# Three feed-forward products of a transformer kernel, taken as sums of products of rounded parts

## The reference

```
x = x + attn(layernorm(x))          # block A: 16 heads, relative bias, causal
x = x + xattn(layernorm(x), ctx)    # block B and D: 8 heads, attends to ctx
x = x + ffn(layernorm(x))           # block C and the last part: 8 experts, one per row
...
y = y @ Wo + x                      # in attn
z = _rms_norm(y, ln2_w)
z = jax.nn.relu(z @ W1) @ W2        # W1 256x1024, W2 1024x256
return z + y
...
ffn = jax.nn.relu(q_enh @ ffn_w1 + ffn_b1) @ ffn_w2 + ffn_b2   # in xattn
```

## Time and profile before

| | us |
|---|---|
| median of 3 runs | 1431.43 (1429.8 to 1434.38) |
| the profiled execution, own time | 1430.63 |
| its span, first to last instruction | 1428.8 |
| PE busy | 1275.9 (89%) |
| DVE busy | 766.8 (54%) |
| ACT busy | 583.0 (41%) |
| POOL busy | 390.7 (27%) |

### The profile page before, as it was taken

How to read it: one execution, slowest core, us unless ns; L and a number is a source line. 1 busy time by engine, 2 the same in 40 slices (tenths; PEclk the granted TensorE clock), 3 DMA queues, 4 the chain that set the end, 5 groups by cost and what they waited for, 6 DMA issues and landing times.

```text
span 1428.8 us, 27261 instructions
## 1 busy us (share of the span) xinstructions
PE 1275.9 (89%) x8838; PEld 929.8 (65%) x8839; DVE 766.8 (54%) x2053; ACT 583.0 (41%) x1253; POOL 390.7 (27%) x680
## 2 busy tenths in 40 slices
PE   6588999999999999999999999999987449999997
PEld 4365776767777776767777777767765325555554
DVE  5645566676766666676666666676643241121111
ACT  3424436363545536363544536363522212222221
POOL 2311121212141221213141221213122124444443
PEclk9598999999999999999999999999999669999999
DMA  8300000000000000000000000000054002112111
GB/s 273 97 8 9 16 1 31 1 29 0 29 29 0 29 0 29 0 29 0 29 29 0 29 0 29 0 29 22 2 192 177 30 22 62 53 56 60 59 55 38
DMA packets 44135, 56.69 MB, mean 40 GB/s; under 512 B 6486, under 2 KB 38016, under 8 KB 44097
## 3 DMA queue, kind: packets, MB, share of 16 engines
q1 hardware_dynamic: 37824, 41.23, 8.8%
q0 software_dynamic: 5616, 14.43, 3.5%
q10 hardware_dynamic: 656, 0.52, 0.1%
HBM read 40.44 MB, written 16.65 MB: 40 GB/s over the span
## 4 chain that ended last, share of the span: by engine, by line
PE 75%; DVE 10%; ACT 8%; issue 5%; POOL 1%; DMA 0%; ACTq 0%; DVEq 0%; SPq 0%; POOLq 0%
PE bank L1337 69%; PE bank L1372 2%; ACT a_p L725 2%; ACT shared L730 2%; PE bank L1519 2%; DVE a_p L1140 2%; DVE shared L1114 1%; PE bank L1664 1%; DVE a_sq L1108 1%; ACT shared L759 1%; ACT b_qh L659 1%; DVE a_split L1084 0%; DVE a_split L1083 0%; DVE shared L1291 0%; DVE a_split L1082 0%
## 5 line engine op out<-in xcount | busy, mean ns | idle before, releaser
L1337 PE MATMUL bank<-shared 128*128 128x256 f32 (+4 forms) x2242 | 447.8, 380 | 44.9 <-ACT shared L670 13.8
L1337 PEld LDWEIGHTS bank<-shared 128*128 128x128 f32 (+2 forms) x2242 | 318.1, 173 | 125.5 <-issue 31.5
L1140 DVE TENSOR_TENSOR a_p<-a_p,eb 128x385 f32<-128x385 f32 x256 | 126.2, 556 | 89.5 <-ACT a_p L725 89.5
L1337 PE MATMUL bank<-up,shared 128*128 x312 | 144.5, 606 | 11.0 <-issue 11.0
L725 ACT ACTIVATE a_p<-bank 128x385 f32<-128x385 f32 x256 | 105.1, 503 | 42.0 <-PE bank L1337 41.9
L869 POOL TENSOR_SCALAR a_rz<-a_ms 128x2 f32<-128x2 f32 x16 | 3.1, 191 | 431.7 <-ACT a_sq L736 431.7
L1337 PE MATMUL bank<-a_xnT,w 128*128 128x256 f32 x512 | 114.7, 382 | 1.4 <-ACT a_xnT L622 1.4
L1337 PE MATMUL bank<-w,a_hT 128*128 128x256 f32 x512 | 113.1, 379 | 0.0
L1314 DVE TENSOR_TENSOR shared<-bank,shared 128x512 f32<-128x512 f32 x39 | 27.0, 692 | 154.4 <-ACT shared L757 84.7
L622 ACT COPY a_xnT<-bank 128x512 f32<-128x512 f32 x32 | 18.8, 587 | 220.2 <-PE bank L1372 220.2
L1337 PEld LDWEIGHTS bank<-a_xnT,w 128*128 128x128 f32 x512 | 96.0, 190 | 18.1 <-issue 3.4
(11 more groups left out here) (206 smaller groups left out, 2037.9 us busy)
## 6 DMA issues: line engine op xcount, KB each, us to landing
up<-in_L_ffn_up_w SPq DMA_DIRECT2D x8, 1024.0 KB, 14.4
x_in<-in_x SPq DMA_DIRECT2D x16, 256.0 KB, 2.7
shared<-in_ctx SPq DMA_DIRECT2D x16, 256.0 KB, 3.0
rows_x<-shared SPq DMA_DIRECT2D x16, 256.0 KB, 2.9
rows_skip<-shared SPq DMA_DIRECT2D x16, 256.0 KB, 3.1
down<-in_L_ffn_down_w SPq DMA_DIRECT2D x8, 512.0 KB, 12.5
toep<-a_hT SPq DMA_DIRECT2D x1, 3072.0 KB, 10.2
eb<-toep SPq DMA_DIRECT2D x4, 512.0 KB, 6.2
```

Source lines behind the costliest of these rows:

```text
L1140: tt(a_p[:, n_ % NPA], a_p[:, n_ % NPA], eb[:, n_], ALU.mult).then_inc(sig["a_p"], 1)
L1337: return mm(out, lhsT=lhsT, rhs=rhs, start=first, stop=last, **kw)
```

## The change

W1 and W2 of block A (w01, w02) and the first feed-forward weight of the cross block (w11) are split into a float32r part (`w_hi`) and a rest (`w_low`), likewise their inputs (`a_zT`, `a_hT`, `d_qT`), and each float32 product becomes three float32r products, from turn 3 on (SPLIT_FROM = 3). `w12` stays as it is.

- The weights' high parts are written over the weights themselves. There is no room to keep the rests: they are computed once in turn 2 in scratch room (`made0`, `a_hT_low`), stored to DRAM, and loaded again in every turn, 1024 KB each, into room that is free at that time: w01's rest over the queries and keys, w02's over `a_p`, w11's over `b_p`.
- Setup: ACT rounds two weights aside in turn 2 ahead of its scores (2048 columns each), the third at the end of turn 2, then writes w11's high part (two halves); at the head of turn 3 it waits until all three rests are stored; ahead of the scores of turn 3 it writes the high parts of w01 and w02 (four halves). DVE computes the rests after ACT has rounded.
- In each turn DVE gets six more operations, 128x512 each: the rest of `d_qT`, of `a_zT` and of the four pieces of `a_hT` (the last with the ReLU in the same instruction). ACT's operations on these jobs now write the high parts. The bank is freed by DVE.
- A.h0 to A.h3 get four banks (1, 2, 3, 0) in place of two.

```diff
-    add((2, 3), [f"A.h{n}" for n in range(4)])
+    add((1, 2, 3, 0), [f"A.h{n}" for n in range(4)])
+SPLIT = ("w11", "w01", "w02",)
+SPLIT_FROM = 3
...
# SP, in turn
+            if it.first == SPLIT_FROM - 1:
+                for n, name in enumerate(SPLIT):
+                    sp.wait_ge(s_low, n + 1)
+                    sp.dma_start(low_of[name].ap(), made_low[n % 2].bitcast(F32)).then_inc(s_low_out[name], 16)
+                for name in SPLIT:
+                    sp.wait_ge(s_low_out[name], 16)
...
+            if "A" in it.stages and it.first >= SPLIT_FROM:
+                full(sp, it, f"A.s{H0 - 1}")
+                sp.dma_start(flat(w01_low[:]).bitcast(F32), low_of["w01"].ap()).then_inc(s_low_in["w01"], 16)
+                after(sp, "a_p_used", it.batch("A"))
+                sp.dma_start(flat(w02_low[:]).bitcast(F32), low_of["w02"].ap()).then_inc(s_low_in["w02"], 16)
+            if "B" in it.stages:
+                after(sp, "b_p_used", it.batch("B"))
+                sp.dma_start(flat(w11_low[:]).bitcast(F32), low_of["w11"].ap()).then_inc(s_low_in["w11"], 16)
...
# ACT
+        def round_aside(which):
+            for n in which:
+                if n == 0:
+                    act.wait_ge(s_w, 4 * C + 3)
+                if n == 2:
+                    act.wait_ge(s_low_out[SPLIT[0]], 16)
+                copy(made_low[n % 2], flat(weight[SPLIT[n]][:])).then_inc(s_hi, 1)
+        def round_in_place(names):
+            act.wait_ge(s_low, len(SPLIT))
+            for name in names:
+                for half in range(2):
+                    part = slice(half * HID, (half + 1) * HID)
+                    copy(flat(weight_hi[name][:])[:, part], flat(weight[name][:])[:, part]).then_inc(s_round, 1)
...
+            if it.first == SPLIT_FROM:
+                for name in SPLIT:
+                    act.wait_ge(s_low_out[name], 16)
             if A:
                 evacuate(it, "A.xn", a_xnT[:].rearrange("p c s -> p (c s)"))
...
+            if it.first == SPLIT_FROM - 1:
+                round_aside((0, 1))
+            if it.first == SPLIT_FROM:
+                round_in_place(SPLIT[1:])
             for what, st, n in PLAN:
...
# DVE
+        def low_parts(which):
+            for n in which:
+                dve.wait_ge(s_hi, n + 1)
+                tt(made_low[n % 2], flat(weight[SPLIT[n]][:]), made_low[n % 2].bitcast(F32), ALU.subtract).then_inc(s_low, 1)
+        def rest(it, job, dst, hi, name, n=None):
+            ps = full(dve, it, job)
+            first = SPLIT_FROM - 1 if name[0] == "a" else 0
+            wait(dve, sig[name], (it.batch("D" if name == "d_qhi" else "A") - first) * PER_BATCH[name] + (n or 1))
+            if n:
+                ins = dve.scalar_tensor_tensor(flat(dst), ps[:], 0.0, flat(hi).bitcast(F32), ALU.max, ALU.subtract)
+            else:
+                ins = tt(flat(dst), ps[:], flat(hi).bitcast(F32), ALU.subtract)
+            ins.then_inc(e_sem(job), 1)
...
# PE
+        def split_cols_out(it, job, xT, xT_low, w, w_low, first_chunk, hi_ready=None):
+            ps = claim(pe, it, job)
+            for m in range(2):
+                at = slice((first_chunk + m) * P, (first_chunk + m + 1) * P)
+                for c in range(C):
+                    product(ps[:, m * S:(m + 1) * S], w[:, c, at], xT[:, c, :], c == 0, False)
+                for c in range(C):
+                    product(ps[:, m * S:(m + 1) * S], w_low[:, c, at], xT[:, c, :], False, False)
+                if m == 0 and hi_ready:
+                    taken(pe, it, hi_ready)
+                for c in range(C):
+                    ins = product(ps[:, m * S:(m + 1) * S], w[:, c, at], xT_low[:, c, :], False,
+                                  c == C - 1)
+            ins.then_inc(f_sem(job), 1)
...
+                        if it.first >= SPLIT_FROM:
+                            product(out, a_hT_hi[:, j, tok(t)], w02_hi[:, j, :], j == 0, False)
+                            product(out, a_hT_hi[:, j, tok(t)], w02_low[:, j, :], False, False)
+                            ins = product(out, a_hT_low[:, j, tok(t)], w02_hi[:, j, :], False, j == J - 1)
```

More of the change, by code:

```diff
@@ L45 @@
 TILES_MAX = NT + E - 1
-SHARED = 22980
+SHARED = 23040
 QUARTERS = 4
@@ L238, in _build @@
     s_fold = sem("bias_through_hidden_weights")
-    shared = sbuf(ctx, "shared", [P, SHARED])
+    b_kh, b_kl, b_qh, b_ql = (sbuf(ctx, name, [P, C, S], F32R) for name in ("b_kh", "b_kl", "b_qh", "b_ql"))
+    b_nmT = sbuf(ctx, "b_nmT", [P, C, S], F32R)
+    whole_shared = ExitStack()
+    shared = sbuf(whole_shared, "shared", [P, SHARED])
+    place = {}
     def carver():
@@ L351, in _build, with doubles @@
[L351 to L354, removed]
+    def doubles(stack, sizes, wanted):
+        made, at = {}, 0
+        for name, words in sizes:
+            if name not in wanted:
+                sbuf(stack, f"under_{name}", [P, words])
+                continue
+            alias, shape = wanted[name]
+            made[alias] = sbuf(stack, alias, shape, F32R)
+            if words > C * HID and name != "made0":
+                sbuf(stack, f"above_{name}", [P, words - int(np.prod(shape[1:]))])
+        return made
@@ new lines, in _build @@
+    starts = sorted((place[name], name) for name in place)
+    sizes = [(name, nxt - at) for (at, name), (nxt, _) in zip(starts, starts[1:] + [(SHARED, None)])]
+    at_f = [name for name, _ in sizes].index("b_f")
+    sizes[at_f:at_f + 3] = [("made0", C * HID)]
+    whole_shared.close()
+    r1 = doubles(ctx, sizes, {
+        "w11": ("w11_hi", [P, C, HID]), "b_zT": ("d_qT_hi", [P, C, S]), "b_yT": ("d_qT_low", [P, C, S]),
+        "b_p": ("w11_low", [P, C, HID]), "b_hT": ("a_hT_low", [P, J, S]), "made0": ("made0", [P, C, HID])})
@@ L466, in _build @@
     pa.close()
+    pr = ExitStack()
+    r2 = doubles(pr, in_pa, {
+        "w01": ("w01_hi", [P, C, HID]), "w02": ("w02_hi", [P, J, D]), "a_xnT": ("a_zT_hi", [P, C, S]),
+        "a_qk": ("w01_low", [P, C, HID]), "a_p": ("w02_low", [P, J, D]), "a_yT": ("a_zT_low", [P, C, S]),
+        "a_hT": ("a_hT_hi", [P, J, S])})
+    w01_hi, w02_hi, a_zT_hi, w01_low, w02_low, a_zT_low, a_hT_hi = (r2[n] for n in (
+        "w01_hi", "w02_hi", "a_zT_hi", "w01_low", "w02_low", "a_zT_low", "a_hT_hi"))
+    weight = {"w01": w01, "w02": w02, "w11": w11}
+    weight_hi = {"w01": w01_hi, "w02": w02_hi, "w11": w11_hi}
+    low_place = {"w01": w01_low, "w02": w02_low, "w11": w11_low}
+    pr.close()
     up = sbuf(ctx, "up", [P, E, C, 2 * EH])
@@ L1156, in turn @@
                 taken(dve, it, "B.wo")
+            if A and it.first >= SPLIT_FROM:
+                rest(it, "A.z", a_zT_low[:], a_zT_hi[:], "a_zhi")
+            if Bb:
                 stats(b_q, b_st, b_mv2, "b_stats2", "b_mv2", b)
@@ L1164, in turn @@
                 shifted(b_q, b_q, b_mv2, b_rs2[:, 1], "b_q")
+            if A and it.first >= SPLIT_FROM:
+                rest_of_hidden(it, (2,))
             if Dd:
@@ L1592, in turn @@
             if A:
-                taken(pe, it, "A.z")
+                if it.first == SPLIT_FROM:
+                    pe.wait_ge(s_round, 2 * len(SPLIT))
+                if it.first >= SPLIT_FROM:
+                    wait(pe, sig["a_zhi"], a - (SPLIT_FROM - 1) + 1)
+                    wait(pe, s_low_in["w01"], (a - (SPLIT_FROM - 1)) * 16 + 16)
+                else:
+                    taken(pe, it, "A.z")
                 if it.first == 1:
```

135 lines of the change are left out of this document (94 added, 41 removed).

## The result

The changed kernel takes **1531.01 us** (median of 4 runs, 1525.91 to 1532.0); the kernel before took 1431.71 beside it (1429.8 to 1434.38). The ratio is 1.0685, with a 95% interval of 1.0656 to 1.0714. It is slower by 99 us, and outside the predicted range of 1421 to 1446.

A forecast was written before the change was run, and what follows sets the result against it. TensorE, busy in 89% of the span, was taken as the bound, with other chains close behind in tail and head. The profiled 1430.6 us less 19.2 gain plus 22.4 paid once gave 1433.8 us, range 1421 to 1446.

The forecast's parts named there:

- D.q's rest on DVE: In each loop turn, DVE's making of the rest of d_qT was said to fit ahead of `b_kl`; zero cost.
- The price of a product: On TensorE, three float32r products at 0.110 us each: 0.33 us for 0.436, so a job of four saves 0.42 us.
- rival 2: At D.h1 to D.h3, the full-height load is not entirely hidden: 1439 us at 0.12 per product, 1444 at 0.13; chance 0.14.
- Rival 3: In all split products, load and product run in series at 0.22 us: near 1600 us; chance 0.03.
- D.h1 to D.h3: Loop stretch from B.m4 on, bound by TensorE: 1.27 us saved a turn, net 1.17 us.
- D.h0: Beside the chain from B.q_ to the rough scores: its 0.42 us falls into TensorE's 0.96 us wait; zero.
- A.h and A.out: Loop tail: 3.4 us less on TensorE, but 0.48 open and the POOL chain 0.35 later; gain 0.08 us a turn.
- Turn 2: Ahead of its scores, two ACT roundings of 2048 columns, 1.98 us each; cost 4.0 us, once.
- Turn 3: Paid once: 10.7 us until the copy of A.xn, 1.4 for the lowered clock, 4.9 ahead of the scores.
- Turn 18: D.h0 waits for D.q's rest until 1107.1, then four jobs follow, the first at half clock; cost 1.4 us, once.
- Transfers: Three loads of 1024 KB per turn arrive in time; zero, or 1.5 us a turn if they took 14.4 us.
- Rival 1: The loop's tail has more room than read: 1426 us, or 1381 if TensorE bounds throughout; chance 0.21, 0.04 of it for 1381.

The follow-up runs named there:

- bank 7: The changed kernel with D.q moved from bank 2, shared with B.k, to bank 7, that of D.h0; 1449.61 us.
- the new order: ScalarE's scaled rows of C and c_x2 behind B.x's copy, VectorE's D.out statistics ahead of b_q's; 1425.78 us on the kernel before, 1415.82 with bank 7 and D.h's split.
- the best version: The changed kernel with bank 7, the new order on ScalarE and VectorE, and the setup's roundings moved to where ScalarE waited; 1398.29 us.

## Why the prediction was wrong, step by step

**The step that failed** is the line "D.q's rest on DVE fits in front of `b_kl`, where it had waited ... Zero". It asked when the rest's own reader (D.h0) needs it, and that was right: nothing waits for `d_qT_low` as data in the loop. It did not ask what the *source* of the rest holds up. The bank that it reads stays taken until the rest is made, and its next user is B.k, a few us later. This is 81 of the 99 us. In the turn shown it is 5.3 us, 5.0 of waiting and 1.7 of half clock at B.k, less the 1.4 that TensorE otherwise waits ahead of B.q_; on average it is 5.4. The experiments show it from both sides: the bank changed gives 81 us back, and the late release without the products costs the kernel before 64. None of the five rivals was this one. The prediction followed what was queued behind the moved work on its engine, and named a bank of A.qk as a place to watch, but never asked for the bank of D.q, the job that changed hands.

With that step set right (bank 7), the remaining sum can be checked: 1449.6 measured for 1433.8, 15.8 us more.

- *The price of a product*, 0.110 forecast: 0.118, from the rows at 577.09 to 577.33. A job of four saves 0.436 x 4 - 12 x 0.118 = 0.33 us and not 0.42. This is rival 2 in a small form. Rival 3, load and product in series at 0.22, is refuted. The Trainium skill, in TensorE: Matmul & The Clock Gate, Part 3, lets a load overlap only where row groups differ, and here loads and products of the same full height stand 0.118 us apart; the measurement decides.
- *D.h1 to D.h3*, 1.17 a turn forecast: 1.0 between the kernels without and with D.h's split (64.91 to 63.91; 0.94 in the new order). Right, and the shortfall is about 3 x 0.09, the product's price. D.h0 was rightly zero: TensorE now waits 1.37 us ahead of B.m4 where it waited 0.96.
- *A.h and A.out*, +0.08 a turn forecast: -0.8. The mechanism was right: the tail is 2.2 us shorter on TensorE (A.z to A.xn 13.05 us for 15.26), and then it waits: 0.75 ahead of A.qk0, for bank 4, which x1 (L1346) frees on VectorE behind the sums of stage D, and with bank 7 1.44 ahead of B.q_, for the copy of B.x, which stands behind `b_xl`'s chain. The size was wrong: the statistics that POOL waits for end 9.99 us after A.z, where they ended after 8.21 and 9.5 was forecast. POOL begins c_norm at 10.18 for 9.34: 0.84 later, not 0.35, and `b_xl` comes 1.0 us later. The walk gave each rest 0.61 us and let it start where the work ahead of it ended; in the trace VectorE waits for ScalarE's parts of A.h1 (0.63 us) and A.h3 (0.22), and the small excesses add up on a chain that had 0.48 us of room. This is 0.86 us a turn less than forecast, and most of the 15.8. (All in all, the 13 turns from A.z of turn 3 to A.z of turn 16 came 4.3 us shorter than before, for 16.3 forecast.)
- *Turn 2*, 4.0 forecast: 5.3 (from B.k to A.z of turn 2, 47.9 us for 42.6). The two roundings took 1.91 each, and TensorE then also waits 1.0 us for a product of VectorE, in whose stream the rests stand ahead of it.
- *Turn 3*, 17.0 forecast, 15.8 with the turn's own gain of 1.25: with bank 7, 16.1 (from A.z of turn 2 to A.z of turn 3, 79.8 us for 63.7). Right in the sum, with some luck in the parts: 9.5 for 10.7 up to the copy of A.xn (the store took 3.9 us for 4.9, VectorE's rest 2.29 for 2.4), 2.6 for 1.4 for the clock (the eight wide products behind the wait), 3.8 to 3.9 for 4.9 ahead of the scores.
- *Turn 18*, 1.4 forecast: 3.1 (in both kernels 41.5 us from its first transposes to those of turn 19, for 38.4). D.h0 waits for the rest as forecast, but with bank 7 28 of the 48 products behind the wait stood 0.21 us apart, at the lower clock, which lasted over two jobs and not one. Turn 17 gained 1.0 for 1.7.
- *Transfers*: zero, as forecast; TensorE waits for none in the loop, and they land as fast as the first of the earlier trace rows.

```profile
w_low<-low_w SPq DMA_DIRECT2D x44, 1024.0 KB, 4.8
```

- *Rival 1*, that the tail has more room: it has none in this order. But it can be made, and then the 17.5 us are there.

So the forecast of "about no change" was right for the change's arithmetic and the setup, and missed a bank that changes hands: 81 us are in the bank, 12 in the turns of the loop (the tail, and a little the price of a product), 3 in turns 2 and 18, 1 in turns 3 and 17. What bounds the best version now is not settled; its largest wait of TensorE in the loop is 1.4 us a turn for a maximum ahead of B.m4.

## What to carry to other kernels

When a result is to be taken out by two engines instead of one, ask of its bank and not only of its reader: the buffer is free after the later of them, and whoever is next in it waits for everything that stands ahead of that instruction. Where a change cheapens the bounding engine in a stretch that another chain closes, look whether the order on the other engines can be changed along with it: the reorderings that gave 5 us to the kernel before, and nothing in its loop, gave 32 to the changed one, and turned block A's split from 0.8 us a turn lost into 1.4 won. Work that is paid once is still worth placing: the roundings of turn 3 cost it 16 us at one place and nothing at another (79.8 and 62.8 us from A.z to A.z, for 63.7 before).

## What the runs showed of the hardware

- A float32r product of 128x128 weights and 256 columns takes 0.118 us with its own weight load, against 0.436 for the two passes of float32 with theirs, where the granted clock was full; at the lower clock it took 0.21 (turn 18 with bank 7).
- After 5.0 us of waiting TensorE came back at about half clock in each of the 11 turns from 5 to 15 (B.k 3.4 to 3.8 us for 1.89). After the shorter waits it went both ways, in like turns of one kernel: after 2.7 us B.k took 2.9 to 3.8 us in 9 of 11 turns, after 2.5 us (VectorE's rest first) 2.8 to 3.5 us in 3 of 11, and 2.0 us in the others. So one turn does not tell what a wait costs. After 9.3 us the eight wide products at the start of turn 3 took 6.31 us for 3.70.
- Rounding 2048 columns on ScalarE took 1.91 us and making their rest on VectorE 2.29 us, both by the column cheaper than the rows of 1536 and 1024 columns from which they were estimated.
